# The mixer's keys put in front of the values' products of heads 0 and 1 in the first attention

## The reference

```python
# mixer, per sample; y is (positions, width)
q, k, v = proj(Wq), proj(Wk), proj(Wv)            # einsum('nclh,dc->ndlh') + bias
ew, ek = exp(w_bias * local_mask), exp(k)
num = einsum('ts,nsd->ntd', ew, ek * v)
den = einsum('ts,nsd->ntd', ew, ek)
y = sigmoid(q) * num / den
h = layernorm(y @ out_w + out_b + flatten(x)) * ln_g + ln_b
# first attention, 16 heads, keys of 16, values of 64
q, k, v = l2norm(q), l2norm(k), l2norm(v)         # from layernorm(h) with the class token in front
attn = square(relu(einsum('bhid,bhjd->bhij', q, k)))
out = tanh_norm(einsum('bhij,bhjd->bhid', attn, v))
h = h + out @ Wout
```

## Time and profile before

| | |
|---|---|
| median of 3 runs | 3464.66 us |
| the profiled execution's own time | 3462.68 us |
| its span, first to last instruction | 3460.9 us |
| TensorE busy | 3069.7 us, 89% |
| VectorE busy | 2102.5 us, 61% |
| ScalarE busy | 1413.4 us, 41% |
| GpSimd busy | 1180.0 us, 34% |
| mean granted TensorE clock | 0.954 |

### The profile page before, as it was taken

How to read it: one execution, slowest core, us unless ns; L and a number is a source line. 1 busy time by engine, 2 the same in 40 slices (tenths; PEclk the granted TensorE clock), 3 DMA queues, 4 the chain that set the end, 5 groups by cost and what they waited for, 6 DMA issues and landing times. The chain is left out here.

```text
span 3460.9 us, 68583 instructions
## 1 busy us (share of the span) xinstructions
PE 3069.7 (89%) x22960; PEld 2311.0 (67%) x22961; DVE 2102.5 (61%) x5152; ACT 1413.4 (41%) x2884; POOL 1180.0 (34%) x1028
## 2 busy tenths in 40 slices
PE   3899999999999999999679999999999934999990
PEld 2677667766776677676356766767766724999990
DVE  4666776667677666766346666666666634444442
ACT  1444444444444444444124444444444413444440
POOL 2443344334434443443212222222222221444440
PEclk7999999999999999999789999999999976999995
DMA  3343234324323442343000111111111115444449
GB/s 77 86 98 86 64 93 97 80 69 94 97 73 73 97 97 65 81 97 91 8 28 28 45 42 35 46 43 34 46 41 35 41 57 148 78 77 76 76 77 303
DMA packets 189481, 257.37 MB, mean 74 GB/s; under 512 B 31009, under 2 KB 151138, under 8 KB 189426
## 3 DMA queue, kind: packets, MB, share of 16 engines
q1 hardware_dynamic: 154962, 213.19, 23.7%
q0 software_dynamic: 25936, 34.95, 6.1%
q10 hardware_dynamic: 8528, 8.52, 0.7%
HBM read 142.30 MB, written 114.25 MB: 74 GB/s over the span
## 5 line engine op out<-in xcount | busy, mean ns | idle before, releaser
L661 ACT ACTIVATE R<-psA 128x1024 f32<-128x1024 f32 x256 | 263.1, 1028 | 166.3 <-PE psA L1136 164.0
L847 DVE TENSOR_TENSOR PR<-R 128x1024 f32<-128x1024 f32 x256 | 322.5, 1260 | 0.0
L1151 PE MATMUL psA<-PR,V 128*64 128x258 f32 x2048 | 283.8, 398 | 0.0
L1868 DVE TENSOR_REDUCE m_nm<-psC 128x4 f32<-128x516 f32 (+1 forms) x256 | 238.9, 955 | 71.3 <-PE psC L2140 70.7
L66 POOL TENSOR_TENSOR vrn<-vsm,inv_root 128x16 f32<-128x16 f32 x64 | 185.5, 2899 | 276.7 <-DVE vsm L832 273.2
L666 ACT ACTIVATE oTs<-psA 128x258 f32<-128x258 f32 x256 | 98.7, 386 | 430.8 <-PE psA L1151 428.7
L1739 ACT ACTIVATE m_PT<-psC 128x770 f32<-128x770 f32 x256 | 197.7, 799 | 186.3 <-PE psC L2169 186.3
L1196 PE MATMUL psA<-wout,OT 128*128 128x256 f32 x1024 | 254.2, 392 | 0.4 <-DVE OT L889 0.4
L1656 POOL DMA_INDIRECT xg<-r_tn,r_idx x130 | 127.8, 983 | 281.1 <-DMA xg<-r_tn,r_idx 243.1
L1196 PEld LDWEIGHTS psA<-wout,OT 128*128 128x128 f32 x1024 | 185.7, 191 | 34.4 <-issue 0.9
L66 POOL TENSOR_TENSOR rstd<-rstd,inv_root 128x2 f32<-128x2 f32 x64 | 45.6, 712 | 405.0 <-DVE rstd L745 405.0
(11 more groups left out here) (412 smaller groups left out, 7909.1 us busy)
## 6 DMA issues: line engine op xcount, KB each, us to landing
ks<-kparts SPq DMA_DIRECT2D x256, 128.0 KB, 4.5
qs<-qparts SPq DMA_DIRECT2D x256, 128.0 KB, 4.9
e_x<-xg SPq DMA_DIRECT2D x143, 129.0 KB
xraw<-in_x SPq DMA_DIRECT2D x66, 256.0 KB
qparts<-qh SPq DMA_DIRECT2D x128, 128.0 KB, 2.4
xs<-m_zrow SPq DMA_DIRECT2D x32, 264.0 KB
f_even<-out_rows SPq DMA_DIRECT2D x13, 640.0 KB
f_odd<-xs SPq DMA_DIRECT2D x13, 640.0 KB
```

The costliest lines, as they stand in the source:

```text
L661: act.activation(R[:, p % 2], ps[:, 0:2, :].rearrange("p a (t n) -> p a t n", t=LT), ACT.Relu).then_inc(relu_done, 1)
L847: dve.tensor_tensor(PR[:, p % 2, :, :, 0:L], R[:, p % 2], R[:, p % 2], ALU.mult).then_inc(prob_done, 1)
L1151: last = pe.matmul(ps[64 * hh:64 * hh + 64, 2 + p % 2, 0:QCOLS], V[:, d, t, n * DV:(n + 1) * DV], PR[:, p % 2, hh, t, :], start=False, sto ...
L1868: dve.tensor_reduce(nm[:, t, :, DK], ps[:, 0:4, cols], AX.X, ALU.max, negate=True).then_inc(max_done, 1)
```

## The change

On TensorE, the step `mix_keys(j)` moves from behind `attend(i, d, 0)` to in front of it. No other engine's list changes, nor does any wait: each step keeps its own.

```diff
                 if more:
                     mixer_keys(j, 1)
                 sim(i, 1)
+                if more:
+                    mix_keys(j)
                 attend(i, d, 0)
-                if more:
-                    mix_keys(j)
                 sim(i, 2)
                 if more:
                     mix_values(j)
```

More of the change, by code:

```diff
@@ L1233, in sample @@
                 sim(i, 1)
-                attend(i, d, 0)
                 if more:
                     mix_keys(j)
+                attend(i, d, 0)
                 sim(i, 2)
```

## The result

The changed kernel took 3433.48 us (median of 4 runs, 3426.37 to 3436.97), the kernel before 3465.59 us beside it. The ratio is 0.9904 with a 95% interval of 0.9881 to 0.9927: 32 us faster, where 34.5 us and 3430 us were forecast; the interval runs from 25 to 41 us. The profiled execution of the changed kernel took 3426.37 us, its span 3424.6 us.

What follows compares the result with a forecast made beforehand. TensorE, busy 97.20 of 100 us, was taken as the bound, waiting 1.04 us for GpSimd's V in 27 samples. Savings of 34.5 us from the profiled 3462.68, plus 1.98 to the median, gave 3430 us; range 3424 to 3440.

Steps and rivals of the forecast that it cites:

- The wait is on the path: TensorE's first values' product waits 1.04 us for GpSimd's V; time won there is kept until the next sample.
- Start of mix_keys: In the loop, mix_keys starts 0.43 us after ScalarE's second exponential, bringing a new TensorE wait of 0.10 us.
- attend(0) at 6.44, no wait: On TensorE, attend(0) follows mix_keys by 1.65 us; V is ready 0.65 us early, so its wait vanishes.
- From attend(0) to sim(2), 1.31 us: On TensorE, sim(2) follows attend(0) by 1.31 us and so starts 1.28 us earlier, 1.32 in the neighbour.
- the order of the transitions: On TensorE, mix_keys to a sim takes 1.93 us, 0.28 more than to an attend; the new order saves that.
- VectorE as the bound in one parity (1.20): VectorE, 1.07 us earlier, lets osc start 1.2 us earlier; in the neighbour TensorE's 1.32 decides.
- The sum: 1.26 us in 27 samples, less 0.3, plus 0.8 for the 4 samples without the wait: 34.5 us.
- B: Rival: on TensorE, mix_keys to attend(0) costs what the step to sim(2) does; gain 27 us, 3438; chance 0.10.
- C: Rival: the next sample's sim(0) waits for the queries' transfer, gain given back; 3465 if all is lost; chance 0.05.
- D: Rival: attend(0) held back 0.65 us delays ScalarE, relu(2), prob(2) and attend(2); 20 us slower, 3485; chance 0.03.
- The allowance of 1.7 us for a clock drop: In the range's bounds: a stretch with the clock drop costs 1.7 us and could be missing or occur twice more.
- The rule on loading weights ahead: Skill's rule for TensorE: weights load ahead of running matmuls; read alone, neither transition costs, making the gain 7.6 us smaller.

## Why the prediction was right, point by point

*The wait is on the path.* Right in mechanism, and shown three ways: 1.18 us of period by the change, 0.87 by half of it, 0.91 by an earlier V with the order of before.

*Start of mix_keys, 4.79 with a new wait of 0.10 us.* Measured 4.80. Neither row of waits names L1022, so the tenth stays below what the list shows; the start itself says that it is there: ScalarE's exponential starts at 4.36 and mix_keys 0.44 later, while sim(1), at 4.26, would have let it go 0.43 later, at 4.69.

*attend(0) at 6.44, no wait.* Measured 6.44.

*From attend(0) to sim(2), 1.31 us.* This is the term of the sum that was mis-sized. It measured 1.42 (1032.42 to 1033.84). I took the distance behind an attend that starts after idle time or a sim (1048.45 to 1049.76). Behind a group of full matmuls its first product lasts 0.47 instead of 0.36 us and all that follows comes 0.1 later; the same was to be seen behind mix_values in the earlier trace rows, where attend(1) has 0.47. So sim(2) starts at 7.86 and not at 7.75, and of the 0.28 us that the order of the transitions was to bring, 0.17 came. Why the first product lasts longer there, no run shows.

*VectorE as the bound in one parity (1.20).* Wrong in its cause, though not by much in size. The denominators start 0.08 us before prob(1) is over in the profile (1033.94 against 1034.02), not 0.03 after it, and VectorE's queue is free in time: osc waits 0.18 for the tanh in this parity and 0.47 in the other. The bound is TensorE's own sim(3), relu(3) and the tanh in both, and so the gain is that of sim(2) in both.

*The sum.* With 1.185 us a sample instead of 1.26 the 27 samples give 32.0 us, and with 0.17 instead of 0.28 for the transitions the other 4 give 4 x 0.07 = 0.3; less the 0.3 taken off, 32.0 us. Against the medians 32.1 us were measured. That this is so close to 32.0 is luck: the interval of 25 to 41 us holds the forecast 34.5 and also B's 27, so the times alone would not have shown which term was off; the period and the distances do.

The profiled pair alone would say 36.3 us. The 28 samples from about 195 us on gave 33.9 of it (from 195.97 to 1590.70 before, from 199.90 to 1560.75 after), where 28 x 1.185 is 33.2; the rest is about what the two clock drops cost that only the kernel before had, 0.5 us each. From the start of sample 30 to the experts' first product (L2550, 2898.60 before, 2865.08 after) 3.6 us more came, and 2.8 behind it. Of the 3.6 about 1.2 are sample 30's own, an estimate from the steady samples. I count no more of them as the change's: behind sample 30 the two kernels have the same lists, and over all kernels here the first of these stretches took 1304 to 1315 us and the second 559.5 to 562.3, from one execution to the next. The opening up to 200 us was 3.9 us later in the changed kernel's profile, with the clock granted at 0.90 between 130 and 160 us, where the kernel before had 1.00; 0.9 of it was there by the first product of the mixer, ahead of anything that was changed:

```profile
130.00:160.00 30.00, 29.49 (x160) 20.87 (x159) 15.13 (x31) 15.31 (x31) 17.30 (x11) 0.90 0.57 132
```

*The rivals.* B (1.0 us a sample, 3438) fell, by the distance that it names: from mix_keys to attend(0) it is 1.64 us and not 1.93, and the period fell by 1.18. 0.11 of the 0.28 did not come, but behind attend(0), not where B has it. C (given back at sim(0) by the queries' transfer) fell: that wait is 0.2 us once, as before. D (attend(0) held back decides) does not act at the distance of the change, 0.65 us; pushed back by 3.0 us from its old place it does, by the place described above rather than by attend(2). So the prediction was right that D does not act here, but it looked for D's limit in the wrong place: its slack of 1.4 us was that of attend(2), and the path that gave way first was prob(2), the second inverse and the scales. The allowance of 1.7 us for a clock drop was right for the changed kernel (1.6), and so was the assumption that a drop costs about 1.1 more than before.

*The rule on loading weights ahead* (the Trainium skill, "TensorE: Matmul & The Clock Gate", Step-by-step: what each phase is for). Read alone it makes both transitions free. With sim(2) in front of attend(0), the step onto the 64-row tiles again measured 0.28 us more than the other, and the period grew by 0.19: the measurement decides.

## What to carry to other kernels

Where an engine that is busy 97% of the time waits once per round for a slow helper, look in its own list for a group whose inputs are already there and put it in front of the waiting one; the gain is the wait plus or minus what the changed neighbours cost, and that is read from the same pair of neighbours elsewhere in the trace, including what precedes them. Then name the next wait in line and follow what it depends on: here it was a tanh behind a product that could come earlier, worth another 0.4 us a round. Samples that differ by chance, such as those after a clock drop, show whether a wait is on the path before anything is changed.

## What the runs showed of the hardware that was not expected

A wait can hide another loss: a clock drop cost 0.48 us while TensorE waited for V in each sample, and 1.6 us once it did not. The number of drops between 200 and 1600 us differs between orders and between executions: 2 before, 0 and 1 after, 1 with half of mix_keys in front, 6 with V cut in two and the order of before, 2 with the same cut and the changed order, 2 with sim(2) first, 15 with a wait of 1.42 us at the transposition, 0 with residual moved.

In each drop the clock is granted at 0.50, and the drops begin in two places only. All 14 drops of the kernels other than the one with attend(0) far back begin within attend(7), the last step of a sample, 47.2 to 48.5 us after the sample's first one, where no wait of 0.15 us or more stands in the 6 us ahead. Of the 15 with attend(0) far back, 6 begin in attend(7) and 9 within 0.4 us of the end of the wait of 1.42 us. So that wait brought a second place at which the clock falls. What brings the drops in attend(7), and why the cut V with the order of before has six of them, was not tried by itself and stays open.
